# A graph-transformer layer: linear attention by blocks of nodes, and edge counts dealt out anew over the stages before it

## What is computed

```python
xn = _layernorm(x)
def rgat_conv(x, W, q, k, b, ...):          # branch 1, twice (4 heads, then 1)
    xr = jnp.einsum('nd,rdf->rnf', x, W)
    alpha = leaky_relu(xr[etype, dst] @ q + xr[etype, src] @ k)
    a = softmax of alpha over the edges of each dst
    return segment_sum(a * xr[etype, src], dst) + b
# branch 2: linear attention, 12 heads of 64
q, k, v = xn @ W_qkv + b_qkv ;  phi(x) = where(x > 0, x + 1, exp(x))
kv = sum_n phi(k) v ;  z = sum_n phi(k)
y = (phi(q) @ kv) / max(phi(q) . z, 1e-6)
x = x + rgat(elu(rgat(xn))) + (y @ W_out + b_out)
x = x + ffn_int8(layernorm(x))
```

## Time and profile before

| | us |
|---|---|
| runs | 1946.22, 1953.29, 1955.57 |
| median | 1953.29 |
| profiled execution | 1943.37, its span 1941.6, mean granted clock 0.932 |
| K projection begins | 67.9 |
| key-value sums | 277.2 to 290.7 |
| Q projection | 290.7 to 409.1 |
| attention, with its leading tiles and window | 409.1 to 543.9 |
| output projection | 560.8 to 619.4 |
| mask loop begins | 637.3 |

### The profile page before, as it was taken

The page is one execution under the profiler, slowest core; times in us unless marked ns, Lnnn a source line. Parts: engine busy times, 40 slices in busy tenths (PEclk is TensorE's granted clock), DMA queues, the critical chain, the costliest instruction groups (busy, mean ns, idle before and its releaser), DMA issues.

```text
span 1941.6 us, 37033 instructions
## 1 busy us (share of the span) xinstructions
PE 1720.2 (89%) x10735; PEld 1231.2 (63%) x10736; DVE 1339.6 (69%) x2589; ACT 786.2 (40%) x1048; POOL 288.7 (15%) x302
## 2 busy tenths in 40 slices
PE   2499999999999889778998999994989899999975
PEld 1265677766565556448998999993645455555544
DVE  6877866548711789967888888883167357777776
ACT  2132112312211455427878787864212123333342
POOL 2600000001111010100000000001100013333334
PEclk9899999888789899988999999996989999999988
DMA  5111113222143443244012204013356550111122
GB/s 170 52 45 45 55 51 92 74 87 82 61 158 152 162 139 112 95 136 137 27 54 72 63 27 134 27 60 109 115 170 181 167 211 1 48 48 48 36 80 80
DMA packets 122965, 177.60 MB, mean 91 GB/s; under 512 B 12621, under 2 KB 96469, under 8 KB 122377
## 3 DMA queue, kind: packets, MB, share of 16 engines
q1 hardware_dynamic: 122888, 176.62, 28.1%
HBM read 118.75 MB, written 57.84 MB: 91 GB/s over the span
## 4 chain that ended last, share of the span: by engine, by line
PE 69%; DVE 10%; issue 9%; DMA 5%; ACT 2%; DVEq 2%; SPq 1%; POOL 1%; ACTq 0%; POOLq 0%
PE ps L1874 19%; PE ps L1932 7%; PE ps L1931 7%; PE ps L1662 6%; PE ps L1663 6%; PE ps L1664 6%; PE ps L1680 6%; PE ps L1741 3%; PE ps L1720 3%; DVE tt_junk L1409 2%; DMA xr_d<-ev 1%; PE ps L1793 1%; DVE oh_p L1288 1%; PE ps L1770 1%; DVE oh_q L1286 1%
## 5 line engine op out<-in xcount | busy, mean ns | idle before, releaser
L1874 PE MATMUL ps<-xrh,pf 128*128 (+1 forms) x2400 | 406.3, 333 | 30.6 <-DVE pf L1493 24.6
L1874 PEld LDWEIGHTS ps<-xrh,pf 128*128 128x128 f32 x2400 | 402.6, 194 | 34.3 <-issue 33.5
L1662 PE MATMUL ps<-w_hi,xt_hi 128*128 128x384 f16 x960 | 321.8, 335 | 31.6 <-DVE ev L1524 17.5
L1663 PE MATMUL ps<-w_lo,xt_hi 128*128 128x384 f16 x960 | 321.8, 335 | 0.0
L1664 PE MATMUL ps<-w_hi,xt_lo 128*128 128x384 f16 x960 | 321.1, 334 | 0.0
L1286 DVE TENSOR_SCALAR oh_q<-pat,codeT,neg_w 125x630 f16<-125x630 uint16 x420 | 206.2, 491 | 56.9 <-PE ps L1680 43.2
L1931 PE MATMUL ps<-x,ph 128*128 (+1 forms) x600 | 196.5, 327 | 19.4 <-POOL pl L873 19.4
L1493 DVE SCALAR_TENSOR_TENSOR pf<-vb,CT 128x1260 f32<-128x1260 f32 x120 | 175.5, 1468 | 54.4 <-PE ps L1874 54.4
L1932 PE MATMUL ps<-x,ph 128*128 (+1 forms) x600 | 197.8, 330 | 0.0
L1489 DVE SCALAR_TENSOR_TENSOR vb<-vb,tb 128x1260 f32<-128x1260 f32 x120 | 174.4, 1468 | 32.6 <-ACT vb L1067 31.6
L795 POOL TENSOR_TENSOR w_lo<-wst,w_hi 128x2304 f16<-128x2304 f32 x20 | 91.9, 4599 | 684.6 <-ACT w_hi L893 655.7
(11 more groups left out here) (231 smaller groups left out, 2316.0 us busy)
## 6 DMA issues: line engine op xcount, KB each, us to landing
qbc<-tq_d SPq DMA_DIRECT2D x12, 1260.0 KB, 5.8
wst<-in_L_gnn_W SPq DMA_DIRECT2D x12, 1152.0 KB, 6.9
xr_d<-ev SPq DMA_DIRECT2D x60, 192.0 KB, 2.0
xrh<-xr_d SPq DMA_DIRECT2D x4, 2880.0 KB, 15.6
x_d<-ev SPq DMA_DIRECT2D x60, 192.0 KB, 2.3
x<-x_d SPq DMA_DIRECT2D x3, 3840.0 KB, 12.3
mb_d<-mb SPq DMA_DIRECT2D x30, 310.1 KB
mb<-mb_d SPq DMA_DIRECT2D x30, 310.1 KB
```

What stands on the lines that cost most here:

```text
L1662: pe.matmul(ps[:, bank, 0:CW], a_hi, hi[:, k, :], start=(k == 0), stop=False)
L1663: pe.matmul(ps[:, bank, 0:CW], a_hi, lo[:, k, :], start=False, stop=False)
L1874: mm = pe.matmul(out[b], pf[j][:, b * DB:b * DB + P], x, start=(first and b % 2 == 0), stop=False, skip_group_check=True)
```

## The change

1. GpSimdE's ten additions to X go. The two bias rows are loaded behind the loads for the Q projection and summed by GpSimdE behind its sixth weight split; VectorE makes the ten additions behind the attention, before it copies the node columns.
2. Windows: 10 and 20 in the K and V projections as before, 3 (`W_S`) among the key-value sums, behind every second head pair, 18 (three a slice) in the Q projection, one before the attention, and 8 in it.
3. The attention runs over ten blocks of 128 nodes (`weighted(i)`): the block of phi(q) is stationary, `kvd` moves with 130 columns, the last two of which are the denominators of the pair's two heads. VectorE clamps, inverts 12 numbers per node and multiplies (`normalised`); TensorE transposes the block, ScalarE takes the high half from PSUM, VectorE the low half. `zm`, `spread`, `rbc`, `yv` and GpSimdE's part go. The products of block i + 1 stand behind the transposes of block i and need block i normalised.
4. The counts: windows 2 to 49 are loaded in three pieces during the output projection, 0 and 1 behind the first key product, 50 to 59 behind the last; the mask loop waits for the last piece only in its middle. The second weight chunk of the next projection is loaded behind these pieces. Some tiles change their place.

```diff
-        W_K, W_V, W_Q, W_A = 0, 2 * (NB // 2), 6 * (NB // 2), 6 * (NB // 2) + 2 * K6 + 1
-
-        def att_window(n):
-
-            return W_A + n - n // 4 if n % 4 != 3 and W_A + n - n // 4 < NWN else None
+        W_K, W_V, W_S, W_Q = 0, NB, 3 * NB, 3 * NB + 3
...
+        W_A = W_Q + 3 * K6 + 1
+
+        def block_windows(i):
+
+            return range(W_A + i, min(W_A + i + 1, NWN))
+
+        def block_tiles(i):
+
+            t = WT_TILES // 2 + 3
+            return range(t + 2 * i, t + 2 * i + 2) if i < 5 else range(t + 5 + i, t + 6 + i)
+
+        assert W_A + NB >= NWN and block_tiles(NB - 1)[-1] == WT_TILES - 1
...
-            sp.dma_start(bsum[:, :], bo.unsqueeze(0).to_broadcast([P, D])).then_inc(bias_in, 16)
-            sp.dma_start(b2_bc0[:, :], b2.unsqueeze(0).to_broadcast([P, D])).then_inc(bias_in, 16)
...
             chunk_load(7)
+            for k in range(3):
+                store_window(sp, W_S + k, cb, k % 2)
...
+            sp.dma_start(bsum[:, :], bo.unsqueeze(0).to_broadcast([P, D])).then_inc(bias_in, 16)
+            sp.dma_start(b2_bc0[:, :], b2.unsqueeze(0).to_broadcast([P, D])).then_inc(bias_in, 16)
...
+            for i in range(NB):
+                for w in block_windows(i):
+                    store_window(sp, w, cc_, (w - W_Q) % 2)
+                for t in block_tiles(i):
+                    if t + 3 < WT_TILES:
+                        wq_load(t + 3)
...
-            for m in range(2):
-                weights_load(sp, m)
-
-            sp.wait_ge(kq_st, 16)
-            sp.wait_ge(y_lo, K6 * NRG + 2)
+            weights_load(sp, 0)
+            sp.wait_ge(y_lo, 2 * NB)
+            sp.wait_ge(xb_done, NB + 1)
             sp.wait_ge(ct_out[0], 16 * 36 + 16)
             sp.wait_ge(ct_out[1], 16 * 24 + 16)
-            for w0 in range(8, NWN, 13):
-                load_windows(sp, w0, w0 + 13, 1)
+            for w0, w1 in ((2, 10), (10, 30), (30, 50)):
+                load_windows(sp, w0, w1, 0)
+            sp.wait_ge(kq_st, 16)
+            weights_load(sp, 1)
...
+            sp.wait_ge(kb_mm, 1)
+            load_windows(sp, 0, 2, 0)
+            sp.dma_start(qr[0:NW, :, :], kq_d[0:R * H, 0:ND].rearrange("a (w d) -> w a d", d=WD)).then_inc(qr_in, 16)
             sp.wait_ge(kb_mm, H)
-            load_windows(sp, 0, 2, 0)
-            load_windows(sp, 2, 8, 1)
-            sp.dma_start(qr[0:NW, :, :], kq_d[0:R * H, 0:ND].rearrange("a (w d) -> w a d", d=WD)).then_inc(qr_in, 16)
+            load_windows(sp, 50, NWN, 1)
...
-            pool.wait_ge(bias_in, 64)
-            pool.tensor_tensor(bsum[:, :], bsum[:, :], b2_bc0[:, :], ALU.add).then_inc(xb_done, 1)
-            pool.wait_ge(xb_done, 1)
-            pool.wait_ge(ln_done, NB)
-            with pool.Fori(0, NB) as i:
-                pool.tensor_tensor(sub(X, i), sub(X, i), bsum[:, :], ALU.add).then_inc(xb_done, 1)
             w_lo_part(2)
             w_lo_part(3)
             w_lo_part(4)
             w_lo_part(5)
+            pool.wait_ge(bias_in, 64)
+            pool.tensor_tensor(bsum[:, :], bsum[:, :], b2_bc0[:, :], ALU.add).then_inc(xb_done, 1)
             w_lo_part(6)
             w_lo_part(7)
 
...
-            for n in range(K6 * NRG):
-                g, p6 = n // K6, n % K6
-                pool.wait_ge(y_hi, n + 1)
-                pool.tensor_tensor(yt_lo[:, p6, g * RG:(g + 1) * RG], yv[n % 2][:, :], yt_hi[:, p6, g * RG:(g + 1) * RG],
-                                   ALU.subtract).then_inc(y_lo, 1)
-
-
-            pool.wait_ge(y_v, K6 * NRG)
+            pool.wait_ge(ct_ev, NWN + 1)
...
+            for k in range(3):
+                window_out(W_S + k, 6, cb, k % 2, (2 * NB, NB, 2 * NB + 1)[k])
+
+            def late_out(w):
+
+                k = w - W_Q
+                window_out(w, 6, cc_, k % 2, k // 2 + (NB + 1 if k % 2 else 2 * NB + 2))
+
             for c in range(2):
-                with act.Fori(0, 3) as fb:
-                    window_out(W_Q + 2 * (3 * c + fb), 6, cc_, 0, 20 + 3 * c + fb)
+                for fb in range(3):
+                    wa = W_Q + 3 * (3 * c + fb)
+                    late_out(wa)
+                    late_out(wa + 1)
...
-            def y_hi_part(n):
-                g, p6 = n // K6, n % K6
-                act.wait_ge(y_v, n + 1)
-                act.activation(yt_hi[:, p6, g * RG:(g + 1) * RG], yv[n % 2][:, :], ACT.Copy).then_inc(y_hi, 1)
...
+            late_out(W_A - 1)
+            act.wait_ge(xb_done, 1)
+
+            for i in range(NB):
+                for hf in range(2):
+                    act.wait_ge(y_tr, 2 * i + hf + 1)
+                    act.activation(yt_hi[:, 3 * hf:3 * hf + 3, i * P:(i + 1) * P], ps[:, 2 + hf, 0:3 * P].rearrange("p (k n) -> p k n", k=3),
+                                   ACT.Copy).then_inc(y_hi, 1)
+                for w in block_windows(i):
+                    late_out(w)
...
-            act.wait_ge(ct_in[0], 16)
-            act.wait_ge(ct_in[1], 16 * 5)
+            act.wait_ge(ct_in[0], 16 * 4)
...
+            count_part(W_S + 1)
+            count_part(W_S + 2)
             dve.wait_ge(kvs_done, 2)
-            dve.memset(kvd[:, :, :], 0.0)
-            dve.memset(zm[:, :, :], 0.0)
-            dve.tensor_copy(spread[:, :, :].rearrange("p k (u n) -> p (k u) n", u=2),
-                            ident[0:2 * K6, 0:2 * K6].unsqueeze(2).to_broadcast([2 * K6, 2 * K6, P // 2])).then_inc(kvd_done, 1)
+            dve.memset(kvd[:, :, :], 0.0).then_inc(kvd_done, 1)
...
                     h0, h1 = 64 * hf, 64 * hf + 64
                     dve.tensor_copy(kvd[h0:h1, p6, h0:h1], ps[h0:h1, 4 + p6 // 3, o + h0:o + h1])
-                    last = dve.tensor_copy(zm[h0:h1, p6, 2 * p6 + hf:2 * p6 + hf + 1], ps[h0:h1, 4 + p6 // 3, o + P:o + P + 1])
+                    last = dve.tensor_copy(kvd[h0:h1, p6, P + hf:P + hf + 1], ps[h0:h1, 4 + p6 // 3, o + P:o + P + 1])
             last.then_inc(kvd_done, 1)
 
-            dve.wait_ge(xb_done, NB + 1)
-            dve.wait_ge(ct_out[0], 16 * 20 + 16)
-            dve.wait_ge(ct_out[1], 16 * 10 + 16)
...
+            count_part(W_Q)
...
-                    count_part(W_Q + 2 * (3 * c + fb) + 1)
+                    for u in range(2):
+                        count_part(W_Q + 3 * (3 * c + fb) + u + 1)
                     for g in range(NRG):
...
-                    count_part(W_Q + 2 * (3 * c + fb) + 2)
...
-            for g in range(NRG):
-                dve.wait_ge(r_mm, g + 1)
-                dve.tensor_scalar(rden[:, g * RG:(g + 1) * RG], ps[0:2 * K6, g, 0:RG], 1e-6, None, ALU.max).then_inc(r_step, 1)
...
-            def invert(g):
-                dve.wait_ge(r_step, g + 1)
-                dve.reciprocal(rden[:, g * RG:(g + 1) * RG], rden[:, g * RG:(g + 1) * RG]).then_inc(r_step, 1)
...
-                for p6 in range(K6):
-                    n = K6 * g + p6
-                    dve.wait_ge(rbc_done, n + 1)
-                    dve.wait_ge(y_lo, n + 1)
-                    dve.tensor_tensor(yv[n % 2][:, :], ps[:, n % 2, 0:RG], rbc[n % 2][:, :], ALU.mult).then_inc(y_v, 1)
-                    if att_window(n) is not None and att_window(n) + 1 < NWN:
-                        count_part(att_window(n) + 1)
...
+                    count_part(W_Q + 3 * (3 * c + fb) + 3)
+
+            def normalised(i):
+
+                dve.wait_ge(y_done, i + 1)
+                for b in range(2):
+                    last = dve.tensor_scalar(rdn[i % 2][:, K6 * b:K6 * b + K6].rearrange("p (k u) -> p k u", u=2),
+                                             ps[:, b, 0:3 * AW].rearrange("p (k n) -> p k n", k=3)[:, :, P:AW], 1e-6, None, ALU.max)
+                last.then_inc(y_den, 1)
+                dve.wait_ge(y_den, 2 * i + 1)
+                dve.reciprocal(rdn[i % 2][:, :], rdn[i % 2][:, :]).then_inc(y_den, 1)
+                dve.wait_ge(y_den, 2 * i + 2)
+                if i >= 2:
+                    dve.wait_ge(y_tr, 2 * i - 2)
+                for b in range(2):
+                    last = dve.tensor_tensor(yn[i % 2][:, CW * b:CW * b + CW].rearrange("p (k u n) -> p k u n", k=3, u=2),
+                                             ps[:, b, 0:3 * AW].rearrange("p (k n) -> p k n", k=3)[:, :, 0:P].rearrange("p k (u n) -> p k u n", u=2),
+                                             rdn[i % 2][:, K6 * b:K6 * b + K6].rearrange("p (k u) -> p k u", u=2).unsqueeze(3).to_broadcast([P, 3, 2, P // 2]),
+                                             ALU.mult)
+                last.then_inc(y_n, 1)
+
+            normalised(0)
+            count_part(W_A)
+            for i in range(NB):
+                if i + 1 < NB:
+                    normalised(i + 1)
+                for hf in range(2):
+                    dve.wait_ge(y_hi, 2 * i + hf + 1)
+                    dve.tensor_tensor(yt_lo[:, 3 * hf:3 * hf + 3, i * P:(i + 1) * P], ps[:, 2 + hf, 0:3 * P].rearrange("p (k n) -> p k n", k=3),
```

(54 more changed lines are left out.)

83 lines of the change are left out of this document (26 added, 57 removed).

## The result

The changed kernel's median is 1896.3 us over four runs (1882.59 to 1910.74), against 1951.6 us for the kernel before; the ratio is 0.973, 95% interval 0.969 to 0.977. Run twice more beside other kernels it gave 1889.2 (four runs) and 1885.1 us (seven runs); over all fifteen runs the median is 1885.1, with twelve of them from 1879.9 to 1894.1 and three from 1907.7 to 1910.7.

A forecast was written before the change was run, and what follows sets the result against it. TensorE, busy 89% of the span, was taken to bound the kernel. Terms of -16 + 6.6 + 14.2 - 44.5 - 4.5 = -44.2 us from the median of 1953.3 gave 1909 us, range 1889 to 1934.

The forecast's parts named there:

- Bias additions: First stage: without GpSimdE's additions to X, the product behind the first window starts sooner; 16 us gained, bounds 10 and 17.
- The rule that spoke against them: Late X additions: VectorE instructions with two SBUF inputs and GpSimdE's SBUF reads block each other; up to 4 us, left out.
- Windows among the sums: Key-value sums: three added windows cost TensorE 6.6 us, VectorE keeping pace; bounds 6.6 and 9.
- Q projection: Six more windows there cost 13.2 us and a late first window about 1 us: 14.2 us, bounds 13.2 and 24.
- Rival B: Q projection: the third window makes VectorE late, a build exposed per slice at low clock, 32 us, 1941; chance 0.10.
- Attention: Attention by blocks: 90.3 us in place of 134.8, 44.5 us gained, with 1.9 us of low clock for each of eight blocks.
- Rival E: Attention blocks: the clock stays high, so 77 becomes 65 us and the kernel 1897; chance 0.07.
- The handing over: Attention blocks that have no window: 4 us for handing over, counted in the blocks' 77 us.
- The old tail: End of the attention stage, behind the blocks: 0.9 us, taken over from the old stage.
- Counts reloaded: Before the first mask: asking for windows 0 and 1 earlier removes ScalarE's wait, 4.5 us gained, bounds 0 and 5.
- The stages behind: Stages behind the changed ones keep their code and only shift in time.
- the signs that were to show it: Among them: key-value stage near 20 us, Q slices near 22, Q projection to node columns near 90, block periods 7.5 to 9.

The follow-up runs named there:

- the single tiles: Changed kernel with a Q projection slice's three weight tiles dealt out singly, one behind each third of its products, from the second slice: 1907.8 us, ratio 0.979.
- the kernel with 128 rows: Kernel before, with spread products of 128 rows (116 of them zero) in place of 12: 1931.0 us against 1946.8, ratio 0.992.

## Why the prediction was right, and where not

The forecast of 1909 took the first three runs of the kernel before as its start, with a median of 1953.3; over all its 39 runs that kernel has a median of 1947.6. The gain itself was 44.2 by the forecast and is 55.3 us by the first medians, 62.5 from 1947.6 to the 1885.1 of all fifteen runs. That the first median, 1896.3, lies in the range, and above its lower end by 7 us, is in part luck: two of those four runs were of the group near 1910, of the fifteen only three.

*Bias additions (-16).* Right in kind, -18.0 in size with the part that it missed. The reading of the earlier trace rows was confirmed: additions in, steps of 1.99 us and the product at 89.74; additions out, 0.44 and 71.72. The missed 2.7 us are the two loads ahead of the weights. The step said where the loads go and gave their way out no price; rule for the next time: price a load that is taken out of the queue ahead of the first weights. The 0.8 us by which the stretch behind is longer wasn't followed up. The late additions cost nothing on the path, as forecast:

```profile
490.07 8.77 DVE L1390 TENSOR_TENSOR X<-X,bsum 128x768 f32<-128x768 f32 x10
...
508.21 0.56 DVE L1400 TENSOR_TENSOR X<-ps,X 128x384 f32 x1 [9.19 <-PE ps L1672]
```

Ten take 8.8 us and not 11.2, and VectorE is idle for 9.2 us before it is needed. The rule that spoke against them found nothing to act on here: GpSimdE's selectors were through at 484.1, before the first addition. GpSimdE's addition of the two bias rows (1.81 us from 290.58) did hold VectorE up: a one-hot step of 0.25 us from 290.62 took 1.81. TensorE did not wait for it, so it cost nothing, as the forecast had it. The same section of the Trainium skill (SBUF — State Buffer, Who interferes with whom) also has VectorE's two-port modes and GpSimdE lock each other out for a whole instruction; the one-hot steps held to the end of a weight split, 4.53 us above, agree with it.

*Windows among the sums (+6.6).* +6.9, right.

*Q projection (+14.2).* +17.3 in this trace, within its bounds of 13.2 and 24. In the repetitions the same stage was 132.5 and 142.0 us, +14.1 and +23.6, so the term is right for the shortest of the three and the clock makes the rest. The slice of 22.0 was measured as 22.1 on average. VectorE was on time but for the first slice (1.3 us) and one window (0.28). Rival B, VectorE late, did not come about here; the single tiles showed how near it was.

*Attention (-44.5, bounds 7 to 57).* -60.7, outside its own bounds; this is the step that failed. Its kinds of work were priced right (7.0 us a block against 6.92). What failed is the sentence that "in the old stage every group of tiles was followed by a window at 1.2 GHz", taken over as 1.9 us for each of eight blocks, 15.2 us. It was already a misreading of the old trace: of the eleven windows behind a tile in the main part of that stage, seven took 3.07 to 3.89 us, and four 2.07 or 2.08, this one among them (a tile, then the window; timeline of the kernel before):

```profile
444.29 1.50 PE L1720 MATMUL ps<-qkn,wt 128*128 128x2 f32 x12
...
445.92 2.07 PE L1680 MATMUL ps<-oh_q,oh_p 125*128 125x315 f16 x14
```

Measured, the low clock costs 0.2 us in block 0, 1.7 in block 1, right behind the first two tiles (periods of 7.12 and 8.58 us), 0.6 in the last tile, and nothing between. Much of the old stage's low clock hung on its spread products of 12 rows, which the change removes, as the kernel with 128 rows shows. Two tiles bring it down at times: in two of seven traces of the same blocks they last 72.2 and 75.2 us, still under the 77 of the forecast. Rival E (0.07) had this, and its 1897 is nearer to the first median, 1896.3, than the forecast. The handing over was 0.97 us and not 4. The clock (12.7 us too much), this (3.0) and 0.8 us in the work itself are the error of the 77 against 60.4 us measured for the blocks; block 0's products and normalising took 4.0 us for 3.5. The old tail was 0.92 us, as forecast. Of the 60.7 us, some 16 are clock, by the means of 0.84 over 125.9 us and 0.94 over 65.3 (twice the missing share is time at the low level, 40 and 8 us, and half of that is lost), and some 20 are the nine windows that moved out, which the stages in front pay. That leaves some 25 us for the rewritten work; this is a difference, and no run shows it by itself.

*Counts reloaded (-4.5).* The wait is gone (the first mask starts at 579.14, right behind ScalarE's last copy), and 4.5 us with it, but only part for the reason given: 1.9 us for asking earlier, 2.6 for the smaller last piece. The stage gained 2.4: the key products fell to 1.2 GHz sooner and took 14.4 us for 12.1.

*The stages behind* shifted only, to 0.2 us. The terms missed by -16.2 (attention), +3.1 (Q projection), -1.2 (early part), +0.3 (the sums) and -0.1 (all behind the attention), in all -14.1 us: the forecast for this execution was 1899, and it took 1885. The direction was safe: the early part and the attention gained 78.7 us together, and the windows in front of the attention cost 24.2. Of the signs that were to show it, the key-value stage near 20 us and slices near 22 us came; the stage from the Q projection to the node columns took 74 us and not 90, with periods of 5.6 to 8.6 us for the blocks with a window and not 7.5 to 9.

## What to carry over

Before charging a low clock to a stage that is rewritten, ask which products stood ahead of its falls, and whether the rewrite keeps them: products with few rows did it here, and padding them with zeros to 128 rows cost nothing but the zeroing. Count how many of its windows ran low before taking a rule over: it was seven of eleven, not all. When windows of work are moved between stages, count the builder's time in each stage, not the multiplier's: 17 windows in the blocks cost 15 us that 8 did not. And a gain on TensorE that is smaller than a change of the clock's level at one place (1.6 to 1.8 us a window) has to be read in the trace, stage by stage, since in the medians it drowns.

## What the runs showed of the hardware

- A product of 12 rows and 320 f32 columns between products of 128 rows was dearer than one of 128 rows at the same clock level: 0.73 us to the next start against 0.54, and the product ahead of it 0.71 against 0.62.
- With spread products of 12 rows the attention stage had a mean clock of 0.84, with 128 rows 0.97; key products of 24 rows took 11.4 to 14.4 us with the clock falling in each of eleven traces, with 128 rows 8.6 us and no fall. At 2.4 GHz six key products take 2.12 us with either number of rows.
- One program gave traces whose Q projection and lead took 141.5, 144.5 and 151.5 us, with the clock's level behind three tiles in a row as the difference. The same blocks, with at most two tiles in a row, took 65.3 to 65.6 us in five traces and 72.2 and 75.2 in two.
- A one-hot step on VectorE waits out a GpSimdE weight split that is under way: 4.53 us in place of 0.24; in the changed kernel it is 3.15 in place of 0.44, ending at 355.85 where the split ends at 355.67, and hidden but for 0.28 us of TensorE's time. One beside GpSimdE's bias addition takes 1.81 us in place of 0.25.
